# Attention of a four-part model: the weighted sum of the values with fp32 transposed probabilities as stationary operand

## Chip, core and metric

One core of a Trainium2 chip runs the whole program in one launch. The metric is the device time of one execution in microseconds; lower is better. The times of the kernel before are from three runs. Its trace is of one further execution.

## The reference

The program is a chain of four parts, each followed by a residual addition and a layer norm, on x of shape (2, 2048, 256): a Mamba layer, a tree-structured feed-forward layer, causal attention with 16 query heads and 4 key/value heads of width 64, and a mixture of 64 experts. The change touches the attention alone:

```python
qg = q.reshape(b, HKV, G, s, D)
scores = jnp.einsum('bkgqd,bkpd->bkgqp', qg, k) * scale
causal = jnp.tril(jnp.ones((s, s), dtype=bool))
scores = jnp.where(causal, scores, jnp.float32(-1e+30))
probs = jax.nn.softmax(scores, axis=-1)
out = jnp.einsum('bkgqp,bkpd->bkgqd', probs, v).reshape(b, H, s, D)
```

Everything is float32. With two sequences there are 32 pairs of sequence and head, called heads below, each with 2048 queries, 2048 keys and D = 64.

## The kernel before

`attention` (line 1081) runs between `qkv`, which leaves queries, keys and values in DRAM, and `route`. Blocks are 128 by 128 (`P`). The 16 query tiles of a head form four bands of four tiles (`BAND`); band s looks at 4(s+1) key blocks. Two units share the work evenly: unit 0 is bands 3 and 0, unit 1 is bands 2 and 1 (`UNITS`; the first of a unit is its long band, the second its short one). A unit has 20 steps (`STEPS`), so the program has 32 heads x 2 units x 20 steps = 1280 steps.

Each engine has its own instruction list, and semaphores, wrapped in `Tally`, order them. The order is written out by hand. In step v of a unit:

- **TensorE** computes one chunk of scores of the *next* unit (`scores`, lines 1282 to 1293: query tile against up to 512 keys, with the fp32r high and low parts of the keys as two matmuls, and on the diagonal a third that adds the mask); it transposes the probabilities of four query tiles against one key block (`turn`, line 1301, up to 4 transposes into one half of `ps_t`); and it adds the key block of step v - 2 into `ps_o` (`weigh`, line 1313).
- `weigh` holds the values as stationary operand, 128 columns: 64 of their fp32r high part, 64 of the low part (`vbuf`). The transposed probabilities move, up to 512 columns, first their high part, then their low part. `ps_o` therefore holds (2 x 64) x 512 sums, transposed.
- At the end of a band, `take` (line 1458) copies `ps_o` to `folding`, and `fold` (line 1324) adds the two halves and turns the result back: four fp32 matmuls with 128x128 of `folding` as stationary operand and the 128x64 doubled identity `idn_2` moving.
- **ScalarE** takes exponentials of a chunk (`exps`, line 1444), which also sums the row into `sums` by an accumulator, and rounds the transposed probabilities to their high part (`high`, line 1452).
- **VectorE** takes the row maximum of a chunk (`peak`, line 1492; `settle`, line 1505, closes a tile), and makes the low part by a subtraction (`low`, line 1512). Only after `low` is a half of `ps_t` free again. `add_up` and `invert` turn the row sums into reciprocals, `normalise` (line 1530) scales a folded band into `ostage`.
- **GpSimd** splits queries, keys and values into high and low parts (`queries`, `keys`, `values`, `set_values`); **SyncE** issues the loads and the stores. Its order within a head is: load the next head's queries, then store four bands, each after its `normalise`.

Scores run one unit ahead of the transposes, exponentials 16 chunks ahead (`LEAD`, `AHEAD`), and the ring of score buffers has 5 places, so `scores` of a chunk waits for the exponentials of the chunk five before it.

Of the kernel before, what the change touches and what calls it, by code (L numbers as in the profile page):

```python
# [12 lines left out]
P = 128  # L13
# [1067 lines left out]
def attention(nc, q_scr, k_scr, v_scr, ident, causal, attn):  # L1081
# [19 lines left out]
    FOLD = [CB * (long + 1) + 2 for long, short in UNITS]  # L1101
    TURNS = STEPS + 2
# [9 lines left out]
    V_ORDER = sorted(range(BANDS), key=lambda b: max(k * STEPS + g for k in range(NU) for g, (s, kb) in enumerate(GROUPS[k]) if kb // BAND == b))  # L1112
    V_USED = [max(k * STEPS + g + 1 for k in range(NU) for g, (s, kb) in enumerate(GROUPS[k]) if kb // BAND == b) for b in V_ORDER]
    NHEADS = BATCH * HEADS
    NGROUPS = BATCH * KV
    assert STEPS % RING == 0 and STEPS % SLOTS == 0 and TURNS % 2 == 0
# [14 lines left out]
    def use(k, g):  # L1131

        return k * TURNS + g + (g > FOLD[k])

    def fold_use(k, short):
        return k * TURNS + (TURNS - 1 if short else FOLD[k] + 1)

# [6 lines left out]
    with ExitStack() as ctx:  # L1144
# [12 lines left out]
        idn_2 = sb("idn_2", [P, HD])  # L1157
# [5 lines left out]
        vstage = sb("vstage", [P, QT, HD])  # L1163
        qbuf = sb("qbuf", [P, QT, P], F32R)
        kbuf = sb("kbuf", [P, 2, 2, LENGTH], F32R)
        vnext = sb("vnext", [P, QT, 2, HD], F32R)
        vbuf = sb("vbuf", [P, QT, 2, HD], F32R)
# [4 lines left out]
        sums = sb("sums", [P, BANDS, BAND, BANDS])  # L1172
        total = sb("total", [P, BANDS, BAND])
        rinv = sb("rinv", [P, BANDS, BAND, 1])
        folding = sb("folding", [P, CW])
# [3 lines left out]
        ps_o = pb("ps_o3", [P, CW])  # L1179
# [8 lines left out]
        high_v = tally("high_v")  # L1188
        v_ready = tally("v_ready")
        v_set = tally("v_set", BANDS)  # L1190
# [7 lines left out]
        f_done = tally("f_done", 2 * NU, 1)  # L1198
        exp_done = tally("exp_done", PER, 1)
        high_t = tally("high_t", PER)  # L1200
        o_ev = tally("o_ev", 2 * NU, 1)
        t_out = tally("t_out", NU * TURNS, 1)
        cmax = tally("cmax", PER)
        m_done = tally("m_done", QT)
        sum_done = tally("sum_done", 2 * NU)
        r_done = tally("r_done", 2 * NU, 1)
        o_out = [tally("o_out%d" % s, 16, 1) for s in range(BANDS)]
        NCONST = 4
# [13 lines left out]
        def _(sp):  # L1222
# [5 lines left out]
            def load_values(first, col):  # L1228
                sp.dma_start(vstage[:, :, :], v_view[:, bass.ds(first, QT), bass.ds(col, HD)]).then_inc(v_ld.sem, 16)
# [10 lines left out]
            for dst, src in ((idn[:, :], ident), (mask[:, :], causal), (idn_2[0:HD, :], ident[0:HD, 0:HD]),  # L1240
                             (idn_2[HD:P, :], ident[0:HD, 0:HD])):
                sp.dma_start(dst, src).then_inc(consts.sem, 16)
            load_values(0, 0)
# [4 lines left out]
            with sp.Fori(0, NGROUPS) as g:  # L1248
# [5 lines left out]
                sp.wait_ge(v_ready.sem, v_ready.at(g))  # L1254
                sp.sem_inc(sp_seen.sem)
                load_values(first_kv, col_kv)
                with sp.Fori(0, GROUP) as j4:
# [18 lines left out]
            sp.wait_ge(v_ready.sem, v_ready.at(NGROUPS))  # L1276
# [4 lines left out]
        def _(pe):  # L1281
# [13 lines left out]
            def turn(hx, k, g):  # L1295
                s, kb = GROUPS[k][g]
                t = use(k, g)
                pe.wait_ge(exp_done.sem, exp_done.at(hx, band_end(k, s)))
                pe.wait_ge(t_out.sem, t_out.at(hx, t - 1))
                for j in range(max(0, kb - BAND * s), BAND):  # L1300
                    last = nc.tensor.transpose(ps_t[:, t % 2, j * P:(j + 1) * P], probs[:, k, place(k, s, j, kb), :], idn[:, :])  # L1301
                last.then_inc(t_done.sem, 1)

            def weigh(hx, group, k, g):
                s, kb = GROUPS[k][g]
                lo = max(0, kb - BAND * s) * P
# [3 lines left out]
                if kb % BAND == 0:  # L1310
                    pe.wait_ge(v_set.sem, v_set.at(group, V_ORDER.index(kb // BAND) + 1))
                for part in range(2):
                    last = nc.tensor.matmul(ps_o[:, lo:], vbuf[:, kb, :, :],  # L1313
                                            probsT[:, g % SLOTS, part, lo:],
                                            start=kb == 0 and part == 0, stop=kb == BAND * s + BAND - 1 and part == 1)
                last.then_inc(pv_done.sem, 1)

            def fold(hx, k, short):

                t = fold_use(k, short)  # L1320
                pe.wait_ge(o_ev.sem, o_ev.at(hx, 2 * k + short + 1))
                pe.wait_ge(t_out.sem, t_out.at(hx, t - 1))
                for j in range(BAND):
                    last = nc.tensor.matmul(ps_t[:, t % 2, j * HD:(j + 1) * HD], folding[:, j * P:(j + 1) * P], idn_2[:, :],
                                            start=True, stop=True)
                last.then_inc(f_done.sem, 1)
# [5 lines left out]
            f_done.credit(pe)  # L1332
# [6 lines left out]
            with pe.Fori(0, NHEADS) as hx:  # L1339
                group = pe.snap(hx // GROUP)  # L1340
                slot = pe.snap(group % 2)
                slot_next = pe.snap(((hx + 1) // GROUP) % 2)
                for k in range(NU):
# [9 lines left out]
                    for v in range(STEPS):  # L1353
# [3 lines left out]
                        if v >= LAG:  # L1357
                            weigh(hx, group, k, v - LAG)
                        if v == FOLD[k]:
                            fold(hx, k, 0)  # L1360
                    weigh(hx, group, k, STEPS - 2)
# [1074 lines left out]
```

## Time and profile before

| | |
|---|---|
| median of 3 runs | 5497.39 us (5492.1 to 5509.06) |
| the profiled execution, its time | 5475.82 us |
| its span | 5473.9 us |
| PE busy in the span | 4460.2 us (81%), 20448 matmul records |
| DVE, ACT, POOL busy | 3664.0, 2835.9, 2034.8 us |
| granted TensorE clock, mean | 0.931 |

PE stands for TensorE's matmuls, PEld for its weight loads, DVE for VectorE, ACT for ScalarE, POOL for GpSimd, SPq for SyncE's queue. A busy PE is not a PE at its peak: each record includes the way through the array, so records overlap. What one matmul costs is read from the distance between starts. A granted clock of 1.00 is 2.4 GHz, 0.50 is 1.2 GHz.

### The profile page before, as it was taken

Reading aid. Unit: us, or ns where it says so; the run is one execution under the profiler, and the core shown is the slowest. Engines: PE = TensorE matmul, PEld = TensorE weight load, DVE = VectorE, ACT = ScalarE, POOL = GpSimd, SP = SyncE. Lnnn points to the kernel's source line nnn. Section 1 sums busy time; section 2 is a strip of 40 time slices with the busy share of each in tenths; the row PEclk is TensorE's granted clock in tenths of the full one; section 3 lists DMA queues with packets and bytes.
Section 4 is the critical chain, followed back from the end, with each engine's and each line's share of the span. In section 5 each row is a group of like instructions: output and inputs, shape, how many; then the busy total and the mean of one; then the engine's idle time right before and its main releaser. Section 6 shows DMA issues by size and latency. Waiting matters only on the chain. (4 is left out here: it accounts for less than half of the span.)

```text
span 5473.9 us, 85675 instructions
## 1 busy us (share of the span) xinstructions
PE 4460.2 (81%) x20448; PEld 3083.6 (56%) x20449; DVE 3664.0 (67%) x7885; ACT 2835.9 (52%) x6802; POOL 2034.8 (37%) x1819
## 2 busy tenths in 40 slices
PE   6877878699997769999999999998554488888860
PEld 2333333266764348888888888886443355555540
DVE  5999999766665668888888888886443222222239
ACT  5777777322221048888888888886111133333420
POOL 5777777400000021212211122121555455555541
PEclk8999999999999989999999999999777799999985
DMA  1000000101114331110101101011111233333348
GB/s 39 12 12 12 12 16 8 62 29 38 34 37 145 122 83 32 37 44 25 44 25 35 43 25 44 25 44 57 57 53 55 76 120 118 123 115 122 117 138 277
DMA packets 279890, 344.02 MB, mean 63 GB/s; under 512 B 122146, under 2 KB 211866, under 8 KB 273644
## 3 DMA queue, kind: packets, MB, share of 16 engines
q1 hardware_dynamic: 238795, 258.23, 15.7%
q0 software_dynamic: 36416, 80.83, 4.8%
q10 hardware_dynamic: 4608, 4.20, 0.2%
q8 instruction: 24, 0.39, 0.0%
q14 instruction: 47, 0.38, 0.0%
HBM read 237.88 MB, written 107.37 MB: 63 GB/s over the span
## 5 line engine op out<-in xcount | busy, mean ns | idle before, releaser
L1512 DVE TENSOR_TENSOR probsT<-ps_t,probsT 128x512 fp32r<-128x512 f32 (+3 forms) x1280 | 780.0, 609 | 136.6 <-ACT probsT L1452 115.7
L1288 PE MATMUL ps_s<-kbuf,qbuf 128*128 (+1 forms) x2602 | 769.6, 380 | 70.9 <-POOL qbuf L1398 35.1
L1444 ACT ACTIVATE probs<-ps_s,negm 128x512 f32<-128x512 f32 (+3 forms) x1297 | 811.4, 626 | 29.4 <-DVE negm L1505 28.4
L1313 PE MATMUL ps_o<-probsT,vbuf 128*128 128x512 f32 (+3 forms) x2560 | 815.4, 402 | 7.0 <-ACT folding L1458 6.2
L1452 ACT ACTIVATE probsT<-ps_t 128x512 fp32r<-128x512 f32 (+3 forms) x1280 | 685.2, 535 | 257.7 <-PE ps_t L1301 234.5
L1492 DVE TENSOR_REDUCE pmax<-ps_s 128x1 f32<-128x512 f32 (+3 forms) x1301 | 778.3, 601 | 48.4 <-PE ps_s L1288 24.1
L1301 PE MATMUL ps_t<-idn,probs 128*128 128x128 f32 x4352 | 695.6, 275 | 13.9 <-DVE probsT L1512 13.9
L445 POOL TENSOR_TENSOR dBx<-u,b_all 128x1024 f32<-128x1024 f32 x256 | 615.8, 2408 | 236.8 <-DVE h L531 226.0
L1396 POOL CAST qbuf<-qstage 128x512 fp32r<-128x512 f32 x132 | 82.8, 628 | 1543.7 <-DMA qstage<-q_scr 1016.0
L1301 PEld LDWEIGHTS ps_t<-idn,probs 128*128 128x128 f32 x4352 | 517.8, 142 | 134.8 <-DVE probsT L1512 40.9
L1288 PEld LDWEIGHTS ps_s<-kbuf,qbuf 128*128 128x128 f32 x2602 | 447.3, 190 | 189.8 <-issue 77.3
L2076 PE MATMUL ps_gu<-w_gu,xT 128*128 x1160 | 452.8, 515 | 94.1 <-ACT xT L2123 92.8
L235 PE MATMUL ps_y<-hc,idn 128*128 128x512 f32 x1024 | 506.6, 618 | 1.5 <-DVE hc L540 1.5
L531 DVE TENSOR_TENSOR_SCAN h<-ps_a,h_in,dBx 128x512 f32<-128x512 f32 x384 | 471.4, 1268 | 11.3 <-ACT ps_a L361 11.3
L361 ACT ACTIVATE ps_a<-delta,neg_a 128x512 f32<-128x512 f32 x512 | 349.4, 688 | 248.2 <-DVE h L531 244.8
L2200 DVE TENSOR_TENSOR hid<-ps_gu,sg 128x192 f32<-128x192 f32 x290 | 103.6, 358 | 558.2 <-ACT sg L2127 484.3
L1313 PEld LDWEIGHTS ps_o<-probsT,vbuf 128*128 128x128 f32 x2560 | 392.4, 192 | 34.3 <-ACT folding L1458 22.2
L2167 POOL DMA_INDIRECT y<-y,place x288 | 283.6, 985 | 301.3 <-ACT y L2136 185.7
L540 DVE TENSOR_TENSOR hc<-h,ps_c 128x1024 f32<-128x1024 f32 x256 | 312.5, 1221 | 33.2 <-PE ps_c L227 14.1
L2090 PE MATMUL ps_y<-w_d,hT 96*128 x1152 | 310.3, 393 | 23.6 <-issue 19.4
L2160 POOL DMA_INDIRECT xr<-x_rows,token x294 | 282.9, 962 | 117.7 <-issue 90.4
L1835 POOL DMA_INDIRECT table<-entry,dest x256 | 248.1, 969 | 199.5 <-DVE dest L1908 127.0
(216 smaller groups left out, 7427.6 us busy)
## 6 DMA issues: line engine op xcount, KB each, us to landing
parts<-y SPq DMA_DIRECT2D x36, 1024.0 KB, 5.2
qstage<-q_scr SPq DMA_DIRECT2D x264, 128.0 KB
w_gu<-W_guT SPq DMA_DIRECT2D x64, 384.0 KB
at<-attn SPq DMA_DIRECT2D x34, 512.0 KB
q_scr<-rot SPq DMA_DIRECT2D x64, 256.0 KB
attn<-ostage SPq DMA_DIRECT2D x128, 128.0 KB, 2.0
w_d<-W_downT SPq DMA_DIRECT2D x64, 192.0 KB
xt<-x_T SPq DMA_DIRECT2D x18, 512.0 KB
```

The lines of the kernel that those rows point to most:

```text
L235: last = nc.tensor.matmul(ps_y[:, i, :], idn[:, :], hc[:, q % 2, i, :], start=n == 0, stop=n == NST - 1)
L361: nc.scalar.activation(ps_a[:, s % RING, :], delta[:, c % 2, d, :], ACT.Exp, scale=neg_a[:, d, n:n + 1]).then_inc(dA_ready.sem, 1)
L445: nc.gpsimd.tensor_tensor(dBx[:, q % DRIVES, :, :], u[:, hv * DH:(hv + 1) * DH, :], b_all[:, n:n + 1, :].to_broadcast((P, DH, TC)), ALU.mu ...
L531: nc.vector.tensor_tensor_scan(h[:, q % 2, i, :], ps_a[:, s % RING, :], dBx[:, q % DRIVES, i, :], 0.0 if first else h_in[:, n, d:d + 1], A ...
L1288: last = nc.tensor.matmul(ps_s[:, u % RING, 0:w], qbuf[:, BAND * s + j, :], kbuf[:, bass.ds(kslot, 1), part, c * CW:c * CW + w], start=par ...
L1301: last = nc.tensor.transpose(ps_t[:, t % 2, j * P:(j + 1) * P], probs[:, k, place(k, s, j, kb), :], idn[:, :])
L1313: last = nc.tensor.matmul(ps_o[:, lo:], vbuf[:, kb, :, :], probsT[:, g % SLOTS, part, lo:], start=kb == 0 and part == 0, stop=kb == BAND * ...
L1444: nc.scalar.activation(probs[:, k, at:at + n, :], ps_s[:, u % RING, 0:n * P], ACT.Exp, bias=negm[:, tile, :], accum_out=sums[:, s, j, c:c ...
L1452: nc.scalar.activation(probsT[:, g % SLOTS, 0, lo:], ps_t[:, t % 2, lo:], ACT.Copy).then_inc(high_t.sem, 1)
L1492: nc.vector.reduce_max(pmax[:, tile, c:c + 1], ps_s[:, u % RING, 0:blocks(s, j, c) * P], axis=mybir.AxisListType.X).then_inc(cmax.sem, 1)
L1512: nc.vector.tensor_tensor(probsT[:, g % SLOTS, 1, lo:], ps_t[:, t % 2, lo:], probsT[:, g % SLOTS, 0, lo:].bitcast(F32), ALU.subtract).then ...
L2076: last = nc.tensor.matmul(ps_gu[:, b, 0:2 * FF], xT[:, b, k, :], w_gu[:, bass.ds(e % WSLOTS, 1), k, :], start=k == 0, stop=k == KD - 1)
```

## The change

Transposed probabilities and values stay fp32. The roles swap: 128x128 of `probsT` is the stationary operand, and the values, 64 columns and a 65th column of ones, move. One step's `weigh` has one matmul for each query tile, and its result lies untransposed in `ps_o` (128 x 4 x 65); the 65th column is the sum of the row's probabilities. `fold`, `low`, `add_up`, the splitting of the values and the accumulator of the exponential go. Even steps are copied out of `ps_t` by ScalarE (`even`), odd ones by VectorE (`odd`), each from a half of its own. `take` copies into one of two buffers `heaped`. The short band of a unit is inverted and normalised in steps 2 and 3 of the following unit. `vbuf` has two places, filled by the DMA itself; the column of ones is set once by GpSimd.

```diff
-        probsT = sb("probsT", [P, SLOTS, 2, CW], F32R)
+        vbuf = sb("vbuf", [P, 2, QT, OW])
+        probsT = sb("probsT", [P, SLOTS, CW])
+        heaped = sb("heaped", [P, 2, BAND, OW])
-        ps_o = pb("ps_o3", [P, CW])
+        ps_o = pb("ps_o3", [P, BAND, OW])
...
-                            sp.wait_ge(t_out.sem, t_out.at(hx, fold_use(k, short) + 1))
+                            sp.wait_ge(n_done.sem, n_done.at(hx, 2 * k + short + 1))
...
+                out = odd_out if g % 2 else even_out
                 pe.wait_ge(exp_done.sem, exp_done.at(hx, band_end(k, s)))
-                pe.wait_ge(t_out.sem, t_out.at(hx, t - 1))
+                pe.wait_ge(out.sem, out.at(hx, copies(k, g) - 1))
...
-                pe.wait_ge(t_out.sem, t_out.at(hx, use(k, g) + 1))
+                pe.wait_ge(out.sem, out.at(hx, copies(k, g)))
                 if kb == 0:
                     pe.wait_ge(o_ev.sem, o_ev.at(hx, 2 * k + (s == UNITS[k][1])))
-                for part in range(2):
-                    last = nc.tensor.matmul(ps_o[:, lo:], vbuf[:, kb, :, :],
-                                            probsT[:, g % SLOTS, part, lo:],
-                                            start=kb == 0 and part == 0, stop=kb == BAND * s + BAND - 1 and part == 1)
+                for j in range(max(0, kb - BAND * s), BAND):
+                    last = nc.tensor.matmul(ps_o[:, j, :], probsT[:, g % SLOTS, j * P:(j + 1) * P],
+                                            vbuf[:, bass.ds(vslot, 1), kb, :], start=kb == 0 and j == 0,
+                                            stop=kb == BAND * s + BAND - 1)
                 last.then_inc(pv_done.sem, 1)
-            def fold(hx, k, short):
...
-                    act.wait_ge(r_done.sem, r_done.at(hx - 1, 2 * k + 2))
...
-                nc.scalar.activation(probs[:, k, at:at + n, :], ps_s[:, u % RING, 0:n * P], ACT.Exp, bias=negm[:, tile, :],
-                                     accum_out=sums[:, s, j, c:c + 1]).then_inc(exp_done.sem, 1)
+                nc.scalar.activation(probs[:, k, at:at + n, :], ps_s[:, u % RING, 0:n * P], ACT.Exp, bias=negm[:, tile, :]
+                                     ).then_inc(exp_done.sem, 1)
...
-                nc.scalar.activation(probsT[:, g % SLOTS, 0, lo:], ps_t[:, t % 2, lo:], ACT.Copy).then_inc(high_t.sem, 1)
+                nc.scalar.activation(probsT[:, g % SLOTS, lo:], ps_t[:, 0, lo:], ACT.Copy).then_inc(even_out.sem, 1)
...
-                act.wait_ge(f_done.sem, f_done.at(hx, n))
-                nc.scalar.activation(folding[:, :], ps_o[:, :], ACT.Copy).then_inc(o_ev.sem, 1)
+                act.wait_ge(n_done.sem, n_done.at(hx, n - 1))
+                nc.scalar.activation(heaped[:, n % 2, :, :], ps_o[:, :, :], ACT.Copy).then_inc(o_ev.sem, 1)
...
-                nc.vector.tensor_tensor(probsT[:, g % SLOTS, 1, lo:], ps_t[:, t % 2, lo:],
-                                        probsT[:, g % SLOTS, 0, lo:].bitcast(F32), ALU.subtract).then_inc(t_out.sem, 1)
+                dve.wait_ge(t_done.sem, t_done.at(hx, k * STEPS + g + 1))
+                dve.wait_ge(pv_done.sem, pv_done.at(hx, k * STEPS + g - SLOTS + 1))
+                nc.vector.tensor_copy(probsT[:, g % SLOTS, lo:], ps_t[:, 1, lo:]).then_inc(odd_out.sem, 1)
...
-                        low(hx, k, v)
+                        if v % 2:
+                            odd(hx, k, v)
+                        if v == 2:
+                            invert(hx + k - 1, (k - 1) % NU, 1)
+                        elif v == 3:
+                            normalise(hx + k - 1, (k - 1) % NU, 1)
```

How the lists move is shown at two places of TensorE. First a full step in the middle of a band. `ps_t` receives the transposes, `ps_o` the weighted sum, `ps_s` the scores. Before:

```order
L1299 REGISTER_ALU
L1301 MATMUL ps_t<-idn,probs 128x128 x4
L1313 MATMUL ps_o<-probsT,vbuf 128x512 x2
L1286 REGISTER_ALU
L1288 MATMUL ps_s<-kbuf,qbuf 128x512 x2
```

After:

```order
L1285 REGISTER_ALU
L1287 MATMUL ps_t<-idn,probs 128x128 x4
L1297 ISA
L1297 MATMUL ps_o<-vbuf,probsT 128x65 x4
L1272 REGISTER_ALU
L1274 MATMUL ps_s<-kbuf,qbuf 128x512 x2
```

Two matmuls of 512 moving columns became four of 65; the order of the three kinds of work is the same, and an instruction that computes the address of the values is new.

Second, the end of unit 0's long band and the start of its short band. Before:

```order
L1313 MATMUL ps_o<-probsT,vbuf 128x128 x2
L1299 REGISTER_ALU
L1301 MATMUL ps_t<-idn,probs 128x128 x2
L1309 REGISTER_ALU
L1313 MATMUL ps_o<-probsT,vbuf 128x512 x2
L1322 REGISTER_ALU
L1324 MATMUL ps_t<-idn,folding 128x64 x4
L1299 REGISTER_ALU
L1301 MATMUL ps_t<-idn,probs 128x128
L1313 MATMUL ps_o<-probsT,vbuf 128x384 x2
```

After:

```order
L1297 MATMUL ps_o<-vbuf,probsT 128x65
L1285 REGISTER_ALU
L1287 MATMUL ps_t<-idn,probs 128x128 x2
L1295 REGISTER_ALU
L1297 MATMUL ps_o<-vbuf,probsT 128x65 x4
L1287 MATMUL ps_t<-idn,probs 128x128
L1297 MATMUL ps_o<-vbuf,probsT 128x65 x3
```

The fold is gone. The first `weigh` of the short band still comes two transposes after the last one of the long band, with the copy of `ps_o` between them on ScalarE.

## Rows read from the trace of the kernel before

**Rows 1.** Windows by stage: us; busy time and records of each engine; clock, DMA

```profile
1950.00:1994.00 44.00, 17.46 (x49) 12.50 (x49) 15.75 (x27) 14.39 (x38) 14.88 (x14) 0.54 0.60 143
1994.00:3798.00 1804.00, 1751.66 (x11010) 1461.51 (x11010) 1563.66 (x3459) 1491.26 (x3970) 342.65 (x320) 1.00 0.14 33
3798.00:4300.00 502.00, 258.25 (x1138) 204.69 (x1138) 195.89 (x1292) 61.92 (x164) 266.77 (x319) 0.75 0.20 61
```

**Rows 2.** Groups by form, 1994 to 3798 us: count, busy us, mean ns, idle before

```profile
L1301 PE MATMUL ps_t<-idn,probs 128*128 128x128 f32 x4352 | 695.6, 275 | 13.9 <-DVE probsT L1512 13.9
L1313 PE MATMUL ps_o<-probsT,vbuf 128*128 128x512 f32 x1792 | 636.1, 436 | 7.0 <-ACT folding L1458 6.2
L1512 DVE TENSOR_TENSOR probsT<-ps_t,probsT 128x512 fp32r<-128x512 f32 x896 | 618.8, 691 | 105.0 <-ACT probsT L1452 84.1
L1444 ACT ACTIVATE probs<-ps_s,negm 128x512 f32<-128x512 f32 x896 | 617.1, 689 | 23.6 <-DVE negm L1505 22.6
L1492 DVE TENSOR_REDUCE pmax<-ps_s 128x1 f32<-128x512 f32 x898 | 608.5, 681 | 27.4 <-PE ps_s L1288 14.4 <-PE ps_s L1292 7.7
L1452 ACT ACTIVATE probsT<-ps_t 128x512 fp32r<-128x512 f32 x896 | 535.2, 597 | 234.3 <-PE ps_t L1301 212.4
...
L1324 PE MATMUL ps_t<-idn,folding 128*128 128x64 f32 x1024 | 131.7, 271 | 0.0
...
L1458 ACT ACTIVATE folding<-ps_o 128x512 f32<-128x512 f32 x128 | 76.1, 595 | 30.2 <-PE ps_o L1313 30.2
L1313 PE MATMUL ps_o<-probsT,vbuf 128*128 128x384 f32 x256 | 75.7, 376 | 0.0
```

**Rows 3.** Timeline of PE in full steps: start us, duration us, records

```profile
3245.94 0.60 PE L1301 MATMUL ps_t<-idn,probs 128*128 128x128 f32 x4
3246.29 0.71 PE L1313 MATMUL ps_o<-probsT,vbuf 128*128 128x512 f32 x2
3246.84 0.63 PE L1288 MATMUL ps_s<-kbuf,qbuf 128*128 x2
3247.31 0.60 PE L1301 MATMUL ps_t<-idn,probs 128*128 128x128 f32 x4
```

**Rows 4.** Timeline around a fold, weight loads and matmuls

```profile
2979.57 0.97 PEld L1324 LDWEIGHTS ps_t<-idn,folding 128*128 128x128 f32 x8 [0.18 <-issue]
...
2979.67 1.01 PE L1324 MATMUL ps_t<-idn,folding 128*128 128x64 f32 x8
2980.51 0.61 PE L1301 MATMUL ps_t<-idn,probs 128*128 128x128 f32 x4
```

**Rows 5.** Timeline of PE in the Mamba part, fp32 matmuls of 512 columns

```profile
1002.61 1.88 PE L235 MATMUL ps_y<-hc,idn 128*128 128x512 f32 x4
```

**Rows 6.** Timeline of PE, narrow steps at the end of a band

```profile
2977.26 0.83 PE L1313 MATMUL ps_o<-probsT,vbuf 128*128 128x384 f32 x4
2977.93 0.63 PE L1288 MATMUL ps_s<-kbuf,qbuf 128*128 x2
```

**Rows 7.** Timeline, second step of a head: PE behind ACT

```profile
2952.51 0.61 PE L1301 MATMUL ps_t<-idn,probs 128*128 128x128 f32 x4
...
2953.24 0.60 ACT L1452 ACTIVATE probsT<-ps_t 128x512 fp32r<-128x512 f32 x1 [1.78 <-PE ps_t L1301]
...
2953.42 0.60 PE L1301 MATMUL ps_t<-idn,probs 128*128 128x128 f32 x4
2953.73 0.47 ACT L1444 ACTIVATE probs<-ps_s,negm 128x256 f32<-128x256 f32 x1
...
2954.43 0.45 PE L1288 MATMUL ps_s<-kbuf,qbuf 128*128 x2 [0.40 <-ACT probs L1444]
```

**Rows 8.** Timeline where the long band of unit 0 ends

```profile
2974.35 0.42 PE L1313 MATMUL ps_o<-probsT,vbuf 128*128 128x128 f32 x2
...
2975.02 0.59 ACT L1458 ACTIVATE folding<-ps_o 128x512 f32<-128x512 f32 x1
...
2975.03 0.44 PE L1301 MATMUL ps_t<-idn,probs 128*128 128x128 f32 x2 [0.26 <-DVE probsT L1512]
...
2975.66 0.73 PE L1313 MATMUL ps_o<-probsT,vbuf 128*128 128x512 f32 x2 [0.19 <-ACT folding L1458]
```

**Rows 9.** Timeline of SyncE's loads and GpSimd's queries, start of a head

```profile
2954.50 5.46 SPq L1233 DMA_DIRECT2D qstage<-q_scr  x8
...
2961.50 1.29 POOL L1398 TENSOR_TENSOR qbuf<-qstage,qbuf 64x512 fp32r<-64x512 f32 x1 [0.18 <-POOL qbuf L1396]
```

More of the change, by code:

```diff
@@ L1100, in attention @@
     PER = NU * STEPS
-    FOLD = [CB * (long + 1) + 2 for long, short in UNITS]
-    TURNS = STEPS + 2
+    HALF = STEPS // 2
+    OW = HD + 1
     BLOCKS = sum(BAND * s + j + 1 for s in UNITS[0] for j in range(BAND))
@@ L1129, in place, with copies @@
         return start + kb
[L1131 to L1136, printed above, removed]
+    def copies(k, g):
+        return k * HALF + g // 2 + 1
     def chunk(k, v, lead):
@@ L1296, in turn @@
                 s, kb = GROUPS[k][g]
-                t = use(k, g)
+                out = odd_out if g % 2 else even_out
                 pe.wait_ge(exp_done.sem, exp_done.at(hx, band_end(k, s)))
-                pe.wait_ge(t_out.sem, t_out.at(hx, t - 1))
+                pe.wait_ge(out.sem, out.at(hx, copies(k, g) - 1))
                 for j in range(max(0, kb - BAND * s), BAND):
-                    last = nc.tensor.transpose(ps_t[:, t % 2, j * P:(j + 1) * P], probs[:, k, place(k, s, j, kb), :], idn[:, :])
+                    last = nc.tensor.transpose(ps_t[:, g % 2, j * P:(j + 1) * P], probs[:, k, place(k, s, j, kb), :], idn[:, :])
@@ L1342, in _ @@
                 slot_next = pe.snap(((hx + 1) // GROUP) % 2)
+                pe.wait_ge(v_ld.sem, (group + 1) * 16)
                 for k in range(NU):
@@ L1357, in _ @@
                         if v >= LAG:
[L1358 to L1361, printed above, removed]
+                            weigh(hx, slot, k, v - LAG)
+                    weigh(hx, slot, k, STEPS - 2)
                     next_scores(LATE)
-                    weigh(hx, group, k, STEPS - 1)
+                    weigh(hx, slot, k, STEPS - 1)
                     for v in range(LATE + 1, STEPS + 1):
                         next_scores(v)
-                    fold(hx, k, 1)
         @block.gpsimd
@@ L1410, in head_queries @@
                         queries(hx + 1, n)
-            for n in range(2):
+            for n in range(BANDS):
                 queries(0, n)
-            values(0)
-            for n in range(BANDS):
-                set_values(0, n)
-            for n in range(2, BANDS):
-                queries(0, n)
+                if n == 1:
+                    nc.gpsimd.memset(vbuf[:, :, :, HD:OW], 1.0).then_inc(ones.sem, 1)
+                    nc.gpsimd.memset(heaped[:, (2 * NU - 1) % 2, :, :], 1.0).then_inc(ones.sem, 1)
             with pool.Fori(0, NGROUPS) as g:
@@ L1421, in _ @@
                 keys(g + 1)
-                after(v_set.sem, v_set.at(g))
-                values(g + 1)
                 with pool.Fori(1, GROUP) as j4:
                     head_queries(pool.snap(g * GROUP + j4))
-                for n, used in enumerate(V_USED):
-                    after(pv_done.sem, pv_done.at(g * GROUP + GROUP - 1, used))
-                    set_values(g + 1, n)
         @block.scalar
@@ L1465, in _ @@
             exp_done.credit(act)
+            even_out.credit(act)
             o_ev.credit(act)
@@ L1563, in _ @@
                     settle(*ahead(STEPS))
-                    normalise(hx, k, 1)
+            invert(NHEADS - 1, NU - 1, 1)
+            normalise(NHEADS - 1, NU - 1, 1)
     nc.clear_and_free_semaphores(sems)
```

110 lines of the change are left out of this document (36 added, 74 removed).

## Prediction

> **What bounds the kernel now.** I read the windows by stage first. Attention's loop is the stretch from 1994 to 3798 us, 1804 of the 5473.9 us of the span, with PE busy for 1751.7 us (97%), DVE for 1563.7 (87%), ACT for 1491.3 (83%), all at a granted clock of 1.00, which is 2.4 GHz [rows 1]. Three engines are that full, so busy time alone does not name the bound. The timeline does. A full step of TensorE is four transposes, two matmuls of the weighted sum, two of scores, and the next step's transposes start 1.37 us after this one's [rows 3]. Inside it no row carries idle time. The work of ACT in a step (exponential 0.69, copy 0.60) and of DVE (maximum 0.68, subtraction 0.69) [rows 2] fits into the same 1.37 us, barely. So TensorE sets the step, and the other two are close behind. They come to the front only where a unit begins or a band ends.
>
> Those places cost, in a head of 56.35 us (1804 / 32, [rows 1]): in the second step of each unit the scores start 1.01 us after the transposes began, where the four transposes themselves need 0.36, so PE lost 0.65 us waiting for the exponential [rows 7], twice a head. Where unit 0's long band ends, the transposes come 0.68 us after the previous sum's start instead of about 0.2, and the next sum 0.63 us after them instead of 0.2: another 0.9 us [rows 8]. With two smaller places of 0.3 us each I put the loss at 2.8 us a head, 91 us in all.
>
> **The price of each TensorE instruction, from distances between starts.** Transposes: (0.60 - 0.27) / 3 = 0.11 us each. A 512-column fp32r matmul: the scores pair takes 0.47 us, and the sum with its preceding transposes 0.90, of which four transposes are 0.44, so 0.46 for the pair: 0.233 each [rows 3]. A pair of 384 and a pair of 256 columns lie 0.67 us before the next scores [rows 6]; less 0.08 us by which the scores of a sum always start late behind their load, that is 0.59 for both. Pairs of 128 columns cost about 0.2 us, the weight loads' own pace.
>
> The new matmul has an exact likeness in the trace. The fold multiplies with 128x128 fp32 stationary and 64 fp32 columns moving; the new sum has 128x128 fp32 stationary and 65. The fold's 1024 records are two for each instruction of the program (32 heads x 4 folds x 4), so an fp32 matmul is two weight loads and two matmuls. Eight loads take 0.97 us, the last of them 0.19: seven distances of 0.111 us [rows 4]. I take **0.112 us a record, 0.223 us a matmul**.
>
> **What goes, what comes, on TensorE.**
> - Comes: as many matmuls as there are transposes, 4352 [rows 2], two records each: 8704 x 0.112 = **+975 us**.
> - Goes: the sums. Full pairs are half of 1792 records [rows 2]: 896 x 0.466 = 417 us. Of each narrow width there are 128 pairs, as the 256 records of 384 columns show [rows 2]: 128 x (0.59 + 0.2) = 101 us. Together **-518 us**.
> - Goes: the fold, 1024 records x 0.112 = **-115 us**.
> - Full step: 4 x 0.11 + 8 x 0.112 + 0.47 = 1.80 us instead of 1.37.
>
> **What lies beside it.** ACT in a pair of steps falls to two exponentials and one copy, 1.98 us, DVE to two maxima and one copy. A plain copy out of `ps_t` is not in the trace on DVE; the rows nearest are the maximum, 0.68, and the subtraction, 0.69, from the same kind of memory, and I take 0.69. That makes 2.05 us for DVE, against 3.6 us of TensorE. Both engines drop from nearly full to little over half, so I cost their removed work (subtraction, accumulator, half of the copies, sums) at nothing: it was covered by TensorE except at the unit's seams, and everything that could take its place is shorter. The same holds for GpSimd's values. The new memsets, tens of elements to 260 a partition, run once. Storing the short band now waits for step 3 of the next unit, and SyncE issues the next head's query loads behind that store. Today they are issued 2.0 us after the head's first transposes and the first half is ready 10 us after these [rows 7, 9]; 5 us later is still far inside the 27 us until the scores of the next head need them. A load of values has a whole group of four heads to land.
>
> **The seams afterwards.** In the second step the chain stays: transposes of step 0, ACT's copy, the exponential, the scores [rows 7]. Only the accumulator's read leaves it, about 0.1 us. I keep 0.55 us, twice a head. At the end of the long band the wait for the subtraction goes, but ACT's copy of `ps_o` (0.59 for 512 columns, perhaps 0.4 for 260) still stands between the last sum of one band and the first of the next, with two transposes as its only cover [rows 8]: about 0.65 us. The fold at a head's end used to cover the loop's branch and its register work; I add 0.25 us for that. Together 2.0 us a head, 64 us instead of 91: **-27 us**.
>
> Sum: 975 - 518 - 115 - 27 = **+315 us**. Bounds: if all seams closed (0.3 us a head instead of 2.0) and the weight loads hid behind scores once in every step (-0.05 us x 1280), it would be 315 - 54 - 64 = +197; if the 65th column (0.43 / 512 us a record [rows 5]), a slower switch between the kinds of matmul (half a record, 0.056 us, a step) and seams as today all came, 315 + 7 + 72 + 27 = +421. I take the sum: the fold's rows are of the same shape and nearest.
>
> The profiled execution took 5475.8 us, 21.6 less than the median of the three runs. On its own time the sum gives 5791; against the median, 5497.4 + 315 = 5812. I forecast **5812 us**. A difference of 0.3% is about what a measurement of this kernel can tell from none.
>
> **A rule against the row.** The trace shows what limits an fp32 matmul of 512 columns: its records lie (1.88 - 0.59) / 3 = 0.43 us apart, the columns streamed twice in a record [rows 5]; at 64 columns the distance is 0.111 [rows 4], twice what an eighth of 0.43 would be, so there the weight load sets the pace. The Trainium skill, "FP8 and Floating Point Precision", section TensorE Precision Notes, counts a true fp32 matmul as four passes. Counted by passes alone, four matmuls of 4 x 65 columns are 1040 columns against 1024 before, so the new sum would cost what the old one did and the fold would be saved. The skill's page "TensorE: Matmul & The Clock Gate", section LDWEIGHTS, has the load take columns / 1.2 ns, which would be 107 ns for 128 columns, an estimate by that page; by that rule, the trace agrees with its 0.111 us.
>
> **The rivals.**
> 1. *Moving columns set the price* (faster). If the loads hide behind streaming, a record costs 0.43 x 65 / 512 = 0.055 us, and 8704 of them 475 us. The sum is 475 - 518 - 115 - 27 = -185: 5312 us. For it: loads do hide behind 512-column matmuls, and in the new order scores stand between. Against it: only one load per change of kind can hide; the fold's eight show the rest bare [rows 4]. It decides below 0.076 us a record, where the sum passes zero. Chance 0.04.
> 2. *The clock falls.* With short streams TensorE does less in the same time. The stretch behind attention has a granted clock of 0.75, but there PE is busy for only half of the time [rows 1]; in attention the transposes, 30% of it, stream as shortly at 1.00. If the mean fell to 0.90, the loop's 2119 us would be 1/0.90 as long: +235, some 6047 us. Chance 0.04.
> 3. *New waits at the seams.* Each half of `ps_t` has one copier, and `heaped` is freed only by a late normalise. If the seams lose 4 us a head instead of 2, +64: 5876 us. Against it: ACT and DVE have over 1.5 us of slack in each pair of steps. Chance 0.12.
> 4. *Seams close and loads hide partly.* 5725 to 5775 us; the idle engines speak for it, the chain at the second step against it. Chance 0.14.
> 5. The forecast, 5775 to 5850 us: 0.66.
>
> **The numbers.** 5720 to 5885 us takes in 3, 4 and 5 and leaves out 1, 2 and the far bounds. Slower by over 0.3%: all but rival 1 and a sliver, 0.95; within 0.3%: 0.01; faster: 0.04.
>
> **What would show it.** In the changed kernel the attention loop should last about 2119 us (66.2 us a head), with 8704 records of 65 columns whose weight loads lie 0.112 us apart, a full step of 1.80 us, DVE and ACT busy for about 60% of the loop, clock 1.00. Other stages should not move. Records 0.055 us apart would be rival 1; a clock below 0.95, rival 2; idle rows in mid-band on PE, rival 3. The forecast is wrong if the loop is shorter than 2030 or longer than 2190 us.

## Result, and the profile after

| | before | after |
|---|---|---|
| median | 5494.75 us (4 runs, 5476.2 to 5509.06) | 5762.93 us (4 runs, 5749.21 to 5772.6) |
| ratio | | 1.0484, 95% interval 1.045 to 1.0519 |
| profiled execution: time, span | 5475.82, 5473.9 us | 5759.67, 5757.9 us |
| attention, first to last instruction | 1837.0 us | 2092.5 us |
| a head of the loop | 56.35 us | 64.37 us |
| route; experts | 514.2; 994.7 us | 523.6; 1016.7 us |

The changed kernel is 268 us slower; +315 was forecast, and 5762.9 us lies in the range of 5720 to 5885. Attention's +255.5 us is the change: 32 heads x 8.02 make 257, and 1 us is saved around the loop. What is left of the difference of the spans, 284 - 255.5 = 28 us, stands in stages whose code is the same; the traces of the runs below, other than the first four, show the experts between 995 and 1053 us and route between 503 and 538 whatever attention was, so it isn't explained any further. "Loop" below is 32 times the median head.

Windows by stage of the changed kernel, to be held against [rows 1]: us, busy time and records of PE, PEld, DVE, ACT, POOL, then clock, DMA share, GB/s.

```profile
1994.00:4054.00 2060.00, 2024.13 (x16099) 1890.34 (x16097) 1239.75 (x2685) 1066.44 (x2043) 289.14 (x268) 1.00 0.12 29
4054.00:4554.00 500.00, 255.90 (x1116) 203.07 (x1116) 191.46 (x1262) 61.20 (x164) 265.85 (x318) 0.73 0.20 61
```

The loop takes 2060 us (2119 forecast) at a clock of 1.00. DVE fell from 87 to 60% and ACT from 83 to 52%, weight loads rose from 81 to 92%: TensorE stands alone now, where three engines were nearly full.

Groups by form from 1994 us on (they answer to [rows 2]). The first group has 8704 records in the whole trace, as forecast; a few lie ahead of the window.

```profile
L1297 PE MATMUL ps_o<-vbuf,probsT 128*128 x8696 | 1107.3, 268 | 10.7 <-ACT heaped L1409 10.7
L1274 PE MATMUL ps_s<-kbuf,qbuf 128*128 x2554 | 816.3, 404 | 20.7 <-ACT probs L1395 20.7
...
L1395 ACT ACTIVATE probs<-ps_s,negm 128x512 f32<-128x512 f32 x895 | 588.9, 686 | 143.7 <-DVE negm L1458 143.7
...
L1403 ACT ACTIVATE probsT<-ps_t 128x512 f32<-128x512 f32 x510 | 304.7, 597 | 603.1 <-PE ps_t L1287 599.4
L1466 DVE COPY probsT<-ps_t 128x512 f32<-128x512 f32 x383 | 262.2, 685 | 0.6
```

The plain copy on DVE takes 0.685 us; 0.69 was borrowed from the subtraction. ScalarE's full-width copies now wait 599 us for TensorE, where they waited 212 before [rows 2].

The timeline of TensorE in two full steps (start, duration, records), beside [rows 3]:

```profile
2959.11 0.60 PE L1287 MATMUL ps_t<-idn,probs 128*128 128x128 f32 x4
2959.55 1.00 PE L1297 MATMUL ps_o<-vbuf,probsT 128*128 x8
2960.36 0.71 PE L1274 MATMUL ps_s<-kbuf,qbuf 128*128 x2
2960.91 0.60 PE L1287 MATMUL ps_t<-idn,probs 128*128 128x128 f32 x4
2961.34 1.00 PE L1297 MATMUL ps_o<-vbuf,probsT 128*128 x8
```

and of its weight loads there:

```profile
2959.44 0.97 PEld L1297 LDWEIGHTS ps_o<-vbuf,probsT 128*128 128x128 f32 x8
2960.33 0.30 PEld L1274 LDWEIGHTS ps_s<-kbuf,qbuf 128*128 128x128 f32 x2
2960.68 0.59 PEld L1287 LDWEIGHTS ps_t<-idn,probs 128*128 128x128 f32 x4
```

2960.91 - 2959.11 is 1.80 us, as forecast. The eight loads have the very 0.97 us of the fold's eight [rows 4]; between their starts the median is 0.112 us.

The second step of a head, PE and ACT (it answers to [rows 7]):

```profile
2955.08 0.60 PE L1287 MATMUL ps_t<-idn,probs 128*128 128x128 f32 x4
...
2955.80 0.60 ACT L1403 ACTIVATE probsT<-ps_t 128x512 f32<-128x512 f32 x1 [1.14 <-PE ps_t L1287]
2955.98 0.60 PE L1287 MATMUL ps_t<-idn,probs 128*128 128x128 f32 x4
...
2956.29 0.94 ACT L1395 ACTIVATE probs<-ps_s,negm 128x256 f32<-128x256 f32 x2
...
2956.90 0.45 PE L1274 MATMUL ps_s<-kbuf,qbuf 128*128 x2 [0.31 <-ACT probs L1395]
```

The chain stayed: from the transposes to the scores 0.92 us where 0.36 do, so 0.56 are lost; 0.55 was forecast. And the end of unit 0's long band (it answers to [rows 8]):

```profile
2982.74 0.34 PE L1297 MATMUL ps_o<-vbuf,probsT 128*128 x2
2982.91 0.39 PE L1287 MATMUL ps_t<-idn,probs 128*128 128x128 f32 x2
2983.20 0.39 ACT L1409 ACTIVATE heaped<-ps_o 128x260 f32<-128x260 f32 x1 [0.58 <-PE ps_o L1297]
...
2983.64 1.11 PE L1297 MATMUL ps_o<-vbuf,probsT 128*128 x8 [0.34 <-ACT heaped L1409]
```

The transposes come 0.17 us after the sum (0.68 before), the next sum 0.73 us after them, of which about 0.5 is the wait for `heaped`.

**Where the price and the time part.** The distances between the first transposes of neighbouring steps, medians over the heads, against the forecast's own prices (full sum 0.89 for 0.466, the three narrow sums of a band's end 1.34 for 0.79, fold 0.89). Steps count from 0: "0: 1" is the second step of unit 0, from its first transpose to that of step 2. "Rest" is what the prices leave over, an estimate of the waiting that went:

| steps (unit: step) | before | after | difference | priced | rest |
|---|---|---|---|---|---|
| the 24 other steps with a full sum | 30.6 | 40.7 | +10.12 | +10.25 | -0.12 |
| 0: 1 and 1: 1, second steps | 3.00 | 2.81 | -0.19 | 0 | -0.19 |
| 0: 15 to 17 | 3.11 | 3.05 | -0.07 | +0.55 | -0.62 |
| 0: 18, 19 | 5.48 | 4.63 | -0.86 | -0.81 | -0.05 |
| 1: 8 | 1.50 | 1.79 | +0.29 | +0.43 | -0.13 |
| 1: 11 to 13 | 3.63 | 3.72 | +0.08 | +0.55 | -0.47 |
| 1: 14 | 2.61 | 1.85 | -0.76 | -0.46 | -0.29 |
| 1: 18, 19 | 4.63 | 4.01 | -0.61 | +0.09 | -0.70 |

The two first steps (0.01 us shorter) are left out. The 24 steps came out as priced to within 0.12 us a head. The rest column adds to -2.6 us a head: the seams gave back 82 us instead of 27.

### The profile page after: what moved, and what is told of

It reads as the page before. It is cut to its first block and busy times, and to the rows that moved or that the text cites. A ratio compares the mean times of both kernels' runs of the same rounds, so it can differ in the third digit from the quotient of the medians.

```text
span 5757.9 us, 91486 instructions
## 1 busy us (share of the span) xinstructions
PE 4749.2 (82%) x25568; PEld 3520.9 (61%) x25569; DVE 3344.9 (58%) x7119; ACT 2413.5 (42%) x4865; POOL 1979.8 (34%) x1767
## 5 line engine op out<-in xcount | busy, mean ns | idle before, releaser
L1297 PE MATMUL ps_o<-vbuf,probsT 128*128 x8704 | 1108.3, 268 | 10.7 <-ACT heaped L1409 10.7
L1297 PEld LDWEIGHTS ps_o<-vbuf,probsT 128*128 128x128 f32 x8704 | 1069.3, 192 | 21.1 <-ACT heaped L1409 18.3
L1274 PE MATMUL ps_s<-kbuf,qbuf 128*128 (+1 forms) x2602 | 833.7, 405 | 62.4 <-POOL vbuf L1375 36.7
L1395 ACT ACTIVATE probs<-ps_s,negm 128x512 f32<-128x512 f32 (+3 forms) x1297 | 754.3, 622 | 148.8 <-DVE negm L1458 148.8
L1403 ACT ACTIVATE probsT<-ps_t 128x512 f32<-128x512 f32 (+1 forms) x640 | 355.0, 555 | 723.9 <-PE ps_t L1287 720.2
L1274 PEld LDWEIGHTS ps_s<-kbuf,qbuf 128*128 128x128 f32 x2602 | 398.3, 193 | 84.6 <-POOL vbuf L1375 37.1
L1466 DVE COPY probsT<-ps_t 128x512 f32<-128x512 f32 (+2 forms) x640 | 371.1, 580 | 65.5 <-PE ps_t L1287 64.1
```

Of the source, the lines that this page charges most:

```text
L1274: last = nc.tensor.matmul(ps_s[:, u % RING, 0:w], qbuf[:, BAND * s + j, :], kbuf[:, bass.ds(kslot, 1), part, c * CW:c * CW + w], start=par ...
L1297: last = nc.tensor.matmul(ps_o[:, j, :], probsT[:, g % SLOTS, j * P:(j + 1) * P], vbuf[:, bass.ds(vslot, 1), kb, :], start=kb == 0 and j == 0,
L1395: nc.scalar.activation(probs[:, k, at:at + n, :], ps_s[:, u % RING, 0:n * P], ACT.Exp, bias=negm[:, tile, :]).then_inc(exp_done.sem, 1)
L1403: nc.scalar.activation(probsT[:, g % SLOTS, lo:], ps_t[:, 0, lo:], ACT.Copy).then_inc(even_out.sem, 1)
L1466: nc.vector.tensor_copy(probsT[:, g % SLOTS, lo:], ps_t[:, 1, lo:]).then_inc(odd_out.sem, 1)
```

## Experiments

The runs come in three groups of four, each on another chip of the same kind. In the first (`cols33`, `cols128`, `r32`, `relief`) the kernel before has a median of 5163.91 us (7 runs), in the second (`swap`, `swap_scores`, `r32_swap`, `all_act`) 5500.36 (23 runs), in the third (`relief_swap`, `noacc`, `after_order`, `onepart`) 5471.54 (7 runs). The four traces of the first group show route at 394 us and the experts at 800 to 845, while their full steps in attention are as long as elsewhere (1.37 us in `relief`, 1.80 in `cols128`). So totals are compared within a group and loops across all. "Left out" below says what a kernel doesn't compute.

### Does the number of moving columns set the price?

`cols33` multiplies the last 33 columns only (half of the values' columns is left out); `cols128` moves 128, of which 64 are ones.

```diff
-                    last = nc.tensor.matmul(ps_o[:, j, :], ..., vbuf[:, bass.ds(vslot, 1), kb, :],
+                    last = nc.tensor.matmul(ps_o[:, j, 32:OW], ..., vbuf[:, bass.ds(vslot, 1), kb, 32:OW],
```

```diff
-        vbuf = sb("vbuf", [P, 2, QT, OW])
+        vbuf = sb("vbuf", [P, 2, QT, P])
-        ps_o = pb("ps_o3", [P, BAND, OW])
+        ps_o = pb("ps_o3", [P, BAND, P])
```

> The changed kernel, but each matmul of the weighted sum moves only 33 of the 65 columns (32 columns of the values and the ones); half of the output is left out. Theory (the weight load sets the price): the records of the sum stay 0.112 us apart, a full step stays 1.79 us, the attention loop stays at 2060 us. Rival A (moving columns set the price, 0.43 us for 512 columns a record): 0.028 us a record, the loop some 700 us shorter. Rival B (load and stream follow each other, half of 0.112 us each): 0.084 us a record, 8704 x 0.028 = 240 us shorter.

> The changed kernel, but each matmul of the weighted sum moves 128 columns instead of 65 (the added 63 are ones and their sums are not used). Theory: 128 columns stream in 0.43 x 128 / 512 = 0.108 us, still no more than the load, so the records stay 0.112 us apart and the loop within 10 us of 2060. Rival A: 0.108 us a record as well, so this run alone does not tell it from the theory, the run with 33 columns does. Rival B (one after the other): 0.056 + 0.108 = 0.164 us a record, the loop 450 us longer.

Measured: loop 2056.1 us (64.25 for the median head) with 33 columns and 2065.9 (64.56) with 128, against 2059.7 with 65; totals 5457.31 and 5417.96 us, one run each, whose 39 us apart come from other stages. The groups of weight loads, of `cols33` and then of `cols128`:

```profile
L1297 PEld LDWEIGHTS ps_o<-vbuf,probsT 128*128 128x128 f32 x8704 | 1069.3, 192 | 16.7 <-ACT heaped L1409 14.1
```

```profile
L1297 PEld LDWEIGHTS ps_o<-vbuf,probsT 128*128 128x128 f32 x8704 | 1070.3, 192 | 21.3 <-ACT heaped L1409 18.5
```

The median distance of two records is 112 ns in both. Four times the columns move the median head by 0.5%. Rival 1 is out: the price is that of the records, each with its weight load. No run changed the width of the stationary operand, so a fixed price of a record that has nothing to do with its load isn't told apart from the load's.

One thing did change with 33 columns: the granted clock, 1.00 in the whole loop of the changed kernel, was 0.50 for a moment between the two units in seven of the 32 heads, and the six of these whose length can be read took 65.5 us instead of 64.25. It is one run, but the fall of the clock that rival 2 named did come with fewer columns; with 65 and with 128 it never showed in the loop.

### Does the number of records set it?

`r32`: both operands of the new sum in fp32r (66 columns). The low parts of probabilities and values are left out.

```diff
-        probsT = sb("probsT", [P, SLOTS, CW])
+        probsT = sb("probsT", [P, SLOTS, CW], F32R)
-                                            vbuf[:, bass.ds(vslot, 1), kb, :], ...
+                                            vbuf[:, bass.ds(vslot, 1), kb, :].bitcast(F32R), ...
```

> The changed kernel, but transposed probabilities are rounded to fp32r when copied and the values are read as fp32r (one part only, no low part), so a matmul of the sum is one record with one weight load; 66 columns move. It leaves out the low parts, so the sum is less precise. Theory: one load of 0.11 us a matmul, 4 x 0.11 = 0.44 us of sum in a full step, the step 1.34 us, the loop 4352 x 0.112 = 487 us shorter, about 1575 us, the whole about 5275 us, which is faster than the kernel before. Rival (the other engines take over before that): DVE needs 2.05 us for its two maxima and copy in two steps, so a floor of some 1.1 us a step is not reached; a loop above 1650 us would mean that they did.

Measured: 4962.23 us, ratio to before 0.961 (0.9592 to 0.9628); 50.12 us a head, loop 1603.9; 4352 records, again 111 to 112 ns apart. TensorE's timeline in a full step:

```profile
2795.04 0.60 PE L1287 MATMUL ps_t<-idn,probs 128*128 128x128 f32 x4
2795.39 0.61 PE L1297 MATMUL ps_o<-vbuf,probsT 128*128 x4
2795.84 0.72 PE L1274 MATMUL ps_s<-kbuf,qbuf 128*128 x2
2796.39 0.60 PE L1287 MATMUL ps_t<-idn,probs 128*128 128x128 f32 x4
```

1.35 us against 1.80: four records fewer at 0.112. But a head has 136 records fewer, 15.2 us at that price, and is only 14.25 us shorter (64.37 - 50.12; a loop of 1575 us was expected): by that price, with TensorE's steps short again, the seams cost 1.0 us a head more than in the changed kernel. With one record a matmul the new order would be 4% faster than before; two of them make it 5% slower.

### What held the seams of the kernel before?

`relief`: the kernel before, VectorE's subtraction on 8 columns (the low part of the others stays zero). `swap`: the kernel before, ScalarE's next exponential ahead of its copy in step 0 of a unit. `swap_scores`: that, and in unit 0 the scores of step 18 ahead of the sum of step 16. `relief_swap`: `relief` and `swap` together. `noacc`: the kernel before without the exponential's accumulator, the sums set to one (the division is left out).

```diff
-                nc.vector.tensor_tensor(probsT[:, g % SLOTS, 1, lo:], ps_t[:, t % 2, lo:],
+                nc.vector.tensor_tensor(probsT[:, g % SLOTS, 1, lo:lo + 8], ps_t[:, t % 2, lo:lo + 8],
```

```diff
+                    next_exps(1)
...
-                        if v:
+                        if v > 1:
```

```diff
+                        if k == 0 and v == LATE:
+                            next_scores(v)
...
-                    next_scores(LATE)
+                    if k:
+                        next_scores(LATE)
```

```diff
-                                     accum_out=sums[:, s, j, c:c + 1]).then_inc(exp_done.sem, 1)
+                                     ).then_inc(exp_done.sem, 1)
```

> The kernel before, but VectorE's subtraction for the low part of the transposed probabilities works on 8 columns instead of up to 512; the rest of the low part is zero. TensorE's list is unchanged. It leaves out most of the low part. Theory (TensorE sets the step, the other engines only cost at the seams): full steps stay 1.37 us, the waits for the subtraction at the ends of bands go, 0.6 to 1.2 us a head, the loop 20 to 40 us shorter than 1803. Rival (with three engines over 80% busy, DVE holds TensorE back in every step): full steps fall to about 1.27 us or less, the loop over 100 us shorter.

> The kernel before, but at the start of each unit ScalarE takes the exponential of step 1 before the copy of step 0 (two instructions change places, TensorE's list stays). Theory (at the seam the chain transposes, copy, exponential, scores holds TensorE up for 0.65 us, twice a head): step 1 of the units falls from 1.40 and 1.60 us by some 0.65 each, the loop from 1803 to about 1762 us, full steps stay 1.37 us. Rival (the time only moves to the next wait for an exponential or a copy): the head stays within 0.3 us of 56.35.

> As the run swap, and in unit 0 TensorE computes the scores of step 18 before the first weighted sum of the short band, not after it, so that they cover the copy of the sums by ScalarE. Theory: another 0.4 us a head, the loop about 1750 us. Rival: what stood behind those scores (the narrow sums of steps 18 and 19) is now uncovered and gives it back: no more than 0.1 us a head beyond the run swap.

> The kernel before with the exponential ahead of the copy in step 0, and the subtraction on 8 of its columns (the low part of the other columns is left at zero). The first alone won nothing lasting (55.97 us a head against 56.35), the second alone 0.43. If copy and subtraction in a row hold the half of ps_t that the second step needs, both together win more than the sum of the two: step 1 of both units falls from 1.40 and 1.60 to under 0.95, and a head to 54.5 to 55.0 us, the full steps staying at 1.37. If the stall belongs to TensorE's own order, a head stays above 55.5 us.

> The kernel before without the accumulator of the exponential (the row sums are left at one, so the result is not divided by them). The forecast took 0.1 us an exponential for the accumulator's read and gave it no share in the full step. If so, full steps stay at 1.37 us, the steps where ScalarE is late get shorter by 0.1 us each, and a head falls from 56.35 to 55.8 to 56.2. If ScalarE sets the pace of the narrow steps (0.69 + 0.09 + 0.60 us a step against 1.37 of TensorE), more goes: a head of 55.5 or less.

| kernel | time, us | a head | 0: 1 | 1: 1 | elsewhere |
|---|---|---|---|---|---|
| before | 5494.75 | 56.35 | 1.40 | 1.60 | |
| `relief` | 5149.25, one run (before there 5163.91) | 55.92 | 1.40 | 1.60 | 0: 17 -0.43, 1: 18 -0.39, 1: 8 -0.13; back 0: 18 +0.26, 1: 19 +0.27 |
| `swap` | 5484.45, ratio 0.9985 (0.9966 to 1.0004) | 55.97 | 1.19 | 1.11 | back 0: 2 +0.04, 1: 2 +0.14, 1: 4 +0.17 |
| `swap_scores` | 5483.46, ratio 0.9974 (0.9955 to 0.9994) | 55.88 | 1.19 | 1.11 | as `swap`; 0: 19 -0.09 |
| `relief_swap` | 5452.55, one run (before there 5471.54) | 55.40 | 0.73 | 0.90 | as `relief`; back 0: 2 +0.46, 1: 2 +0.35 |
| `noacc` | 5528.44, one run (before there 5471.54) | 55.70 | 1.32 | 1.51 | |

I had expected more of `relief` (20 to 40 us off the loop), `swap` (loop 1762) and `swap_scores` (1750): they gave 14 us, 1791 and 1788 us. The timeline of the second step in `swap` says why:

```profile
2941.51 0.60 PE L1301 MATMUL ps_t<-idn,probs 128*128 128x128 f32 x4
...
2941.86 0.42 PE L1288 MATMUL ps_s<-kbuf,qbuf 128*128 x2
2941.95 0.69 DVE L1513 TENSOR_TENSOR probsT<-ps_t,probsT 128x512 fp32r<-128x512 f32 x1 [0.72 <-ACT probsT L1452]
...
2942.70 0.66 PE L1301 MATMUL ps_t<-idn,probs 128*128 128x128 f32 x4 [0.31 <-DVE probsT L1513]
```

The scores no longer wait for the exponential (0.35 us behind the transposes), but now the transposes of step 2 wait for the half of `ps_t` that the subtraction of step 0 frees. Copy and subtraction, 1.3 us in a row, stood behind the exponential as a second chain. With both taken away the seam closes, to 0.73 and 0.90 us, as expected of `relief_swap`. Still that kernel reaches 55.40 us and not 54.5 to 55.0, because ScalarE is late in the very next step:

```profile
2942.01 0.71 PE L1313 MATMUL ps_o<-probsT,vbuf 128*128 128x512 f32 x2
2942.11 0.57 ACT L1444 ACTIVATE probs<-ps_s,negm 128x384 f32<-128x384 f32 x1
...
2942.66 0.60 ACT L1452 ACTIVATE probsT<-ps_t 128x512 fp32r<-128x512 f32 x1
...
2942.91 0.72 PE L1288 MATMUL ps_s<-kbuf,qbuf 128*128 x2 [0.20 <-ACT probs L1444]
2943.14 0.70 ACT L1444 ACTIVATE probs<-ps_s,negm 128x512 f32<-128x512 f32 x1
2943.29 0.17 DVE L1513 TENSOR_TENSOR probsT<-ps_t,probsT 128x8 fp32r<-128x8 f32 x1 [0.38 <-ACT probsT L1452]
2943.47 0.60 PE L1301 MATMUL ps_t<-idn,probs 128*128 128x128 f32 x4
```

ScalarE has an exponential and a copy in every step. `noacc` puts a number on its share. One head of before, and one of `noacc`:

```profile
2951.62:3007.98 56.36, 54.73 (x345) 45.68 (x345) 48.85 (x109) 46.61 (x124) 7.60 (x8) 1.00 0.11 28
```

```profile
2940.51:2996.21 55.70, 54.30 (x345) 45.75 (x345) 48.57 (x109) 43.44 (x84) 7.61 (x8) 1.00 0.10 28
```

ScalarE is busy 3.17 us a head less (0.08 for each of 40 exponentials), and the head is 0.65 us shorter: by 0.08 to 0.09 in both second steps, 0.09 in 1: 8 and 1: 12, 0.07 in 0: 15, 0.13 in 1: 19, and by nothing in full steps. Most of these places have a rest in the table above. (`noacc`'s longer total comes from its experts, 1053 us.) The accumulator alone makes 0.65, the subtraction alone 0.43 of the 2.6 us. `r32` splits the sum another way: it has all that was taken from ScalarE and VectorE but full steps of 1.35 us, and its seams gave back about 1.6 us; the other 1.0 came only with the longer steps of TensorE. How the 1.6 us divide between subtraction, accumulator and the copies that moved, beyond the 0.65 and 0.43, stays open.

### The same seams in the changed kernel

`after_order`: the changed kernel with the two moves of `swap_scores`; it computes everything. `r32_swap`: `r32` with the same moves (low parts left out). `all_act`: the changed kernel with the odd copies on ScalarE too.

```diff
-                        if v % 2 == 0:
-                            even(hx, k, v)
+                        (odd if v % 2 else even)(hx, k, v)
```

> The changed kernel with two calls moved: ScalarE takes the next exponential ahead of its copy in step 0 of each unit, and the scores of step 18 of unit 0 stand ahead of the weighted sum of step 16. If the stalls left in the changed kernel are ScalarE's order alone (0.59 us in step 1 of unit 0, 0.62 in step 1 of unit 1, 0.61 in step 18 of unit 0), a head should fall from 64.4 to about 62.8 us, step 1 of both units from 1.31 and 1.50 to about 0.85 and 0.90, and the program by about 50 us (ratio to before 1.035 to 1.045). If VectorE's single list holds them, as it did in the kernel before, less than 0.3 us a head goes. In both cases it stays slower than the kernel before.

> The fp32r form of the changed kernel (run r32, low parts left out) with both changes of order of the run swap_scores. Theory: its step 1 loses 0.4 and 0.6 us, its step 18 of unit 0 0.6 us, so the head falls from 50.1 to about 48.5 us and the loop from 1604 to about 1555 us. Rival (ACT and DVE, with two thirds of each step, come to the front): the loop stays above 1590 us.

> The changed kernel with one part undone: ScalarE makes all copies of transposed probabilities, VectorE none. Theory (TensorE's weight loads set the step, sharing the copies only matters at the seams): full steps stay 1.79 us, the head grows by 0 to 1 us from 64.4, the loop 2060 to 2090 us. Rival (sharing the copies is what keeps the changed kernel from being slower still): full steps grow above 1.85 us and the loop beyond 2130 us.

Measured: `after_order` 5679.73 us (4 runs), ratio to before 1.0374 (1.0333 to 1.0416), 62.70 us a head; steps 0: 1 and 1: 1 fell from 1.31 and 1.50 to 0.72 and 0.90 with nothing given back, 0: 19 by 0.47. The loop is 53 us shorter than the changed kernel's. Each against the kernel before of its own group, the totals are 208 and 268 us longer, 60 us apart. `r32_swap` 5251.26 us (6 runs), ratio 0.9566 (0.9542 to 0.9589), 48.54 us a head. `all_act` 5785.23 us (one run), 64.60 a head: 0: 18 and 1: 14 grew by 0.13 and 0.11, full steps by nothing. One head of the changed kernel, and one of `after_order`:

```profile
3017.57:3081.95 64.38, 63.39 (x507) 59.19 (x506) 39.63 (x84) 33.43 (x64) 13.99 (x10) 1.00 0.22 49
```

```profile
2995.74:3058.44 62.70, 62.70 (x507) 58.98 (x506) 38.28 (x84) 33.60 (x64) 14.21 (x10) 1.00 0.23 50
```

PE is busy for all of the 62.70 us. The changed kernel therefore lost at least 64.37 - 62.70 = 1.67 us a head at its seams (waits so short that the records cover them would come on top), and the one before, by the prices, 1.67 + 2.6 = about 4.3, an estimate. The two moves that won 0.5 us on the kernel before win 1.67 here.

That the subtraction's chain is gone doesn't explain this alone. At the second steps the move of the exponential wins 0.38 us a head on the kernel before (`swap`), 0.52 with the subtraction cut to 8 columns (55.92 in `relief`, 55.40 in `relief_swap`), and 1.19 in the changed kernel. Nor is it TensorE's longer step: `r32_swap`, with full steps of 1.35 us, has the same second steps of 0.73 and 0.91 and gives nothing back. What both have and `relief_swap` lacks is a ScalarE with one copy in two steps and no accumulator. Which of the two matters more wasn't tried.

### Is half of the streaming worth its price?

`onepart`: the kernel before with the probabilities' high part alone (their low part is left out), the copies shared by ScalarE and VectorE, and the order of `swap` (VectorE still copies one column of the even steps).

```diff
-                for part in range(2):
-                    last = nc.tensor.matmul(ps_o[:, lo:], ..., probsT[:, g % SLOTS, part, lo:],
+                last = nc.tensor.matmul(ps_o[:, lo:], ..., probsT[:, g % SLOTS, 0, lo:],
```

> The kernel before, with the high part of the probabilities alone moving (their low part is left out): one 512-column matmul a step in place of two, even steps copied by ScalarE, odd ones by VectorE, which still copies one column of the even ones. TensorE's full step would be 1.37 - 0.23 = 1.14 us; VectorE has 0.68 + 0.69 in odd steps and about 0.85 in even ones, 1.11 on the mean, ScalarE 1.09. If TensorE sets the step, 1.14 to 1.20 us, a head of 48 to 49 and a program some 240 us shorter than before (ratio about 0.955). If ScalarE and VectorE set it, as their 83 and 87% of before suggest, the step stays at 1.25 or more and a head above 51.

Measured: 5291.09 us (4 runs), ratio 0.9672 (0.9633 to 0.971), 50.83 us a head: neither the 48 to 49 of the one theory nor the "above 51" of the other. The lightest full steps (0: 6, 0: 8, 1: 4) take 1.13 to 1.14 us, TensorE's price to the digit, but 0: 3, 0: 5 and 0: 13 take 1.44 to 1.57. `r32` without any reordering takes 50.12. So with precision put aside, 128 stationary probabilities and 66 moving columns beat 128 stationary values and 512 moving ones, though by little, and not on equal terms: `onepart` keeps the low part of the values and the fold, `r32` has neither. Which hand-over stretches the long steps of `onepart` stays open.

## Why the prediction was right or wrong, point by point

- **What bounds it**: right. TensorE sets the full step before and after; `noacc` and `relief` left it at 1.37 us, `all_act` at 1.80.
- **0.112 us a record, 8704 records**: right, by the median of 112 ns and the full step of 1.80. That the columns don't set it was shown by `cols33` and `cols128`, that the records do by `r32`; that it is the load within the record is argued from the 92% of the loop in which loads run. By the count of passes alone, which the Trainium skill gives on its page "FP8 and Floating Point Precision" (TensorE Precision Notes), four matmuls of 4 x 65 columns would have left the full step near 1.37 us; it measured 1.80, so the measurement speaks against using that count for few columns. The load time worked out from the Trainium skill's "TensorE: Matmul & The Clock Gate" (LDWEIGHTS), an estimate of 107 ns, is near the 112.
- **The sums and the fold that go** (-518, -115): right as far as the full steps and their rest of 0.12 us a head can tell.
- **A DVE copy of 0.69, ACT and DVE at about 60%**: 0.685; 60 and 52%.
- **"With two smaller places of 0.3 us each I put the loss at 2.8 us a head"**: the term that was mis-sized. It was about 4.3 us by the prices. I had read the timeline at the second steps and at the end of unit 0's band, and guessed the rest. Unit 1's ends and its step 8 alone gave back 1.6 us (0.47, 0.29, 0.70, 0.13), more than the 0.6 put down for all small places. A row of before hinted at it: the full-width subtractions had waited 84 us for ScalarE's copies [rows 2], and I didn't ask where.
- **"I cost their removed work at nothing"**: right for the full steps, too general for the narrow ones, where ScalarE's exponential, read-out and copy can last longer than TensorE's step. There removing the accumulator paid 0.65 us and removing most of the subtraction 0.43.
- **The seams afterwards, 2.0 us a head**: 1.67. The second steps cost 0.56 each as forecast, `heaped` 0.5 instead of 0.65, the loop's branch nothing that can be seen. Of the 2.6 - 0.8 = 1.8 us a head that the forecast missed, 1.5 lay in what it took for the loss before and 0.3 in that after.
- **Together**: -82 instead of -27 at the seams makes 342 - 82 = 260 for the loop, where 257 was measured and 315 forecast. The rival that came closest in time is the fourth, "seams close and loads hide partly" (5725 to 5775 us, given 0.14); only its first half is true, for no load hid beyond what was priced. The clock (rival 2) stayed at 1.00; that transposes are 30% of the loop was a little high (4352 x 0.11 us are 27%). Nothing new waited long at the seams (rival 3).
- **Luck in the total**: of the 268 us, 257 are the loop's. The other stages, forecast not to move, added the rest, which brought the total nearer to the forecast than the loop is.

## What to carry to other kernels

Count records with their weight loads, not moving columns, where no more than 128 columns move: here a record cost 0.112 us with 33, 65 or 128 columns, and fp32 operands doubled the records, which made 4% faster into 5% slower. When work is taken from engines that are 83 to 87% busy, don't sum up stalls from two places looked at; list the distance of every step of the period and subtract the price of its instructions, since the places that had not been looked at gave back 1.6 us a head, those looked at 0.9. And a stall can have a second and a third chain just behind the first: the same move in ScalarE's list paid 0.4 us a head by itself, 0.5 with the subtraction cut away, and 1.2 where ScalarE also had half of its copies and no accumulator.

## What the runs showed of the hardware that was not expected

An fp32r record and one of the two records of an fp32 matmul have the same distance, 111 to 112 ns, with 128 stationary columns. The chip of the first group had the same full steps in attention as the others but very different route and experts (394 and 800 to 845 us, where all other traces show 503 to 538 and 995 to 1053), so only runs on one chip can be compared as totals. With 33 moving columns in place of 65 the granted clock fell to 0.50 for a moment in seven of 32 heads, with 65 and 128 in none. ACTIVATION_READ_ACCUMULATOR shows about 0.2 us in the records, but taking 40 of them from a head freed only 0.08 us each of ScalarE's time.
